# Key-value products ahead of the gate passes in the middle periods of an attention and gated-recurrence kernel

## The chip, the cores and the metric

The kernel runs on one core of a Trainium2 chip. The metric is device time in microseconds of one execution; lower is better. A core has five engines that run side by side, each through its own list of instructions in the order written, and that wait for one another by semaphores: TensorE (PE, matrix products, results in the PSUM banks), VectorE (DVE), ScalarE (ACT), GpSimd (POOL) and the DMA queues. TensorE's weight loads are shown apart from its matmuls, as PEld.

## The reference

Eight sequences of 512 rows with 128 features go through linear attention, a residual and a layer norm; then a gated recurrence runs over the eight sequences as its eight time steps, again with residual and norm.

```python
Q = elu(x @ Wq.T + bq) + 1; K = elu(x @ Wk.T + bk) + 1; V = x @ Wv.T + bv
KV = einsum('bnd,bne->bde', K, V)
Z = einsum('bnd,bd->bn', Q, K.sum(axis=1) + 1e-06)
x = layernorm(x + (einsum('bnd,bde->bne', Q, KV) / Z[..., None]) @ Wo.T + bo)
# over the first axis of x, c starts as in_c:
ft = sigmoid(xt @ wf.T + c @ uf.T + bf); it = sigmoid(xt @ wi.T + c @ ui.T + bi)
gt = tanh(xt @ wc.T + c @ uc.T + bc);    c = ft * c + it * gt
# after the last step:
h = tanh(x @ wo.T + c_final @ uo.T + bo)
out = layernorm(x + h)
```

All data are float32. The host only packs and transposes inputs.

## The kernel before

The order of every engine is written out by hand, one function per engine; no scheduler moves anything. The attention of sequence a takes, on TensorE:

- keys(a), into ps_k (line 436; for a below 4 a bias product, line 444), and queries(a), into ps_q (line 450);
- keys_x(a), line 459: the product of k_rows with the input, into small(a), a corner of the second half of ps_ctx (for a = 7 in ps_k). ScalarE copies it out (xk_copy);
- key_values(a), lines 469 and 470: two products that make the key-value matrix in small(a); VectorE adds an epsilon and writes kvo(a);
- context(a), line 479: the queries times kvo(a), into both halves of ps_ctx.

VectorE then takes the reciprocal of Z (reciprocal_z), the residual in four chunks (residual, line 1020; the upper two chunks raise y_small_ok, the lower two y_ok), the statistics, and later the normalised x1 (normalise). TensorE transposes x1(b) into ps_x1 (x1_turned, line 493); ScalarE writes its rounded part x1_hi (x1_high) and a whole copy (x1_whole), VectorE the rest x1_lo (x1_low). The gates of step t are products of a high and a low part: six matmuls on x1_hi and three on x1_lo (gates_x, lines 513 to 522), and three per gate on the state (gate_s, lines 540 to 545, which wait for s_hi from ScalarE and s_lo from GpSimd). ScalarE makes tanh of the forget gate, key_bias (the bias of the next keys), then tanh of the input and the candidate gate. VectorE makes kept_state, new_state, next_state.

The loop periods() runs six times. In one turn stand keys and queries of sequence k, the attention products of a = k - 1, the residual and norm of b = k - 2, and the gates of step t = k - 3. I call the turn in which the gates of step t stand "period t"; period 0 has an order of its own, periods 1 to 3 share one (a = 3, 4, 5), and a closing part written out by hand has the attention of 6 and 7 and the first half of the gates of step 4. From the gates of step 4 on, the 512 columns go in two halves.

TensorE's function keys_x(a) waits for x_rows_in(a), for k_ok(a + 1) and, from a = 1 to 6, for y_small_ok(a), since the corner it writes shares a bank with the context whose upper chunks the residual of a - 1 still reads. key_values(a) waits for xk_ok and k_sum_ok, context(b) for q_ok, kvo_ok and y_ok(b), x1_turned for x1_ok of each chunk, the first gate matmul for x1hi_ok.

Of the kernel before, what the change touches and what calls it, by code (L numbers as in the profile page):

```python
# [41 lines left out]
C = N // D  # L42
DZ = D + 1
H = C // 2
# [38 lines left out]
def build(nc, x, xt, w_kq, w_vo_in, w_gate, w_out, rows, att_row, out):  # L83
    with ExitStack() as ctx:
# [102 lines left out]
        ctx_mm, z_ok, y_ok = sem("ctx_mm"), sem("z_ok"), sem("y_ok")  # L187
# [230 lines left out]
        def _(pe):  # L418
# [28 lines left out]
            def queries(a):  # L447
                if a >= 1:
                    pe.wait_ge(q_relu_ok, a)
                nc.tensor.matmul(ps_q[:], wkq[:, WQ_T * D:(WQ_T + 1) * D], x_cols[:, a].rearrange("p c d -> p (c d)"),  # L450
                                 start=True, stop=True).then_inc(q_mm, 1)

            def keys_x(a):
                pe.wait_ge(x_rows_in[a], 16)
                pe.wait_ge(k_ok, a + 1)
                if 1 <= a < T - 1:
                    pe.wait_ge(y_small_ok, a)
                for c in range(C):
                    mm = nc.tensor.matmul(small(a)[:, 0:D], x_rows[:, a, c], k_rows[:, a % 2, c],  # L459
                                          start=(c == 0), stop=(c == C - 1))  # L460
                mm.then_inc(xk_mm, 1)
# [21 lines left out]
            def x1_turned(b):  # L483
                if b == 0:
                    pe.wait_ge(ident_ok, 1)
                if b >= 1:
                    pe.wait_ge(x1c_ok, b)
                for c in range(C):
                    if c in dve_chunks(b):
                        pe.wait_ge(x1_ok, x1_done(b, c))  # L490
                    else:
                        pe.wait_ge(x1_act_ok, SHARED_LN.index(b) * H + c - H + 1)
                    mm = nc.tensor.transpose(ps_x1[:, c * D:(c + 1) * D], x1[:, b, c], ident[:])  # L493
                mm.then_inc(x1t_mm, 1)
# [32 lines left out]
            def gates_x(k):  # L527
                for g in range(GATES):
                    gate_x_high(g, k)
                for g in range(GATES):  # L530
                    gate_x_low(g, k)

            def gate_s(g, k):

                ps, done = gate_bank[second_half(k)][g], gates[g][1]
                u, last, part = GATES + g, (STEPS[k][0] - 1) % 2, columns(k)
                if k == 1:
                    pe.wait_ge(split_s_lo, 1)
                pe.wait_ge(shi_ok[step_before(k)], 1)
                nc.tensor.matmul(ps[:, part], wgate_hi[:, u], s_hi[:, last, part], start=False, stop=False,  # L540
                                 skip_group_check=True)
                nc.tensor.matmul(ps[:, part], wgate_lo[:, u], s_hi[:, last, part], start=False, stop=False,
                                 skip_group_check=True)
                pe.wait_ge(slo_ok[step_before(k)], 1)
                nc.tensor.matmul(ps[:, part], wgate_hi[:, u], s_lo[:, last, part], start=False, stop=True,
                                 skip_group_check=True).then_inc(done, 1)
# [116 lines left out]
            for k, a, b, t in periods():  # L663
                if a == 0:

                    keys_x(a)
                    keys(k)
                    key_values(a)
                    queries(k)
                    context(a)  # L670
                    continue

                keys(k)
                if a == 1:
                    keys_x(a)
                if a in (2, 3):
                    x1_turned(a - 2)
                queries(k)
                if t == 0:

                    gate_x_high(0, t)
                    keys_x(a)
                    gate_x_low(0, t)
                    gate_x_high(1, t)
                    key_values(a)
                    gate_x_low(1, t)
                    gate_x_high(2, t)
                    gate_x_low(2, t)
                    context(a)
                    continue  # L690
                if t is not None:
                    gates_x(t)
                    keys_x(a)
                    gate_s(0, t)
                key_values(a)
                if a == 1:
                    setup_gates()
                if t is not None:
                    gate_s(1, t)
                    gate_s(2, t)  # L700
                context(a)
                if b >= 2:
                    x1_turned(b)

            keys(7)
            queries(7)
            gates_x(4)
            keys_x(6)
            gate_s(0, 4)
            key_values(6)  # L710
            keys_x(7)
            gate_s(1, 4)
            gate_s(2, 4)
            context(6)
            key_values(7)
            x1_turned(5)
# [40 lines left out]
        def _(act):  # L757
# [102 lines left out]
            for k, a, b, t in periods():  # L860
                if a == 0:
                    xk_copy(a)
                key_exp(k)
                if a == 1:
                    xk_copy(a)
                    act.wait_ge(halved_ok, 1)
                    nc.scalar.activation(wgate_hi[:, GATES:2 * GATES], wgate[:, GATES:2 * GATES],
                                         ACT.Copy).then_inc(split_hi, 1)
                if t is not None and t >= 1:
                    state_high(t - 1)  # L870
                if t is not None:
                    x1_whole(t)
                if a == 2:
                    xk_copy(a)
                query_exp(k)
                if b == 0:
                    first_normalise(b)
                if a == 0:

                    act.wait_ge(gate_in, 16)  # L880
                    nc.scalar.activation(wgate_hi[:, 0:GATES], wgate[:, 0:GATES], ACT.Copy).then_inc(split_hi, 1)
                if a > 2:
                    xk_copy(a)
                if t is not None:
                    forget_tanh(t)
                    key_bias(k + 1)
                    input_tanh(t)
                if b is not None:
                    x1_high(b)

            key_exp(7)
            state_high(3)
            x1_whole(4)
            query_exp(7)
            xk_copy(6)
            forget_tanh(4)
            xk_copy(7)
            input_tanh(4)
# [43 lines left out]
        def _(dve):  # L942
# [128 lines left out]
            def attention_end(b):  # L1071

                residual(b, range(H, C), y_small_ok)
                residual(b, range(H), y_ok)
                dve.wait_ge(y_ok, b + 1)
                dve.wait_ge(y_small_ok, b + 1)
                statistics(b)
                variance(b)
# [18 lines left out]
            for k, a, b, t in periods():  # L1097
                if a == 0:
                    key_values(a)
                    key_max(k)  # L1100
                    continue
                if b < 2:
                    reciprocal_z(b)
                if b == 1:
                    residual(b, range(H, C), y_small_ok)
                    x1_low(0)
                    residual(b, range(H), y_ok)
                    dve.wait_ge(y_ok, b + 1)
                    dve.wait_ge(y_small_ok, b + 1)
                    statistics(b)  # L1110
                    variance(b)
                else:
                    attention_end(b)
                if a == 1:
                    query_sum(a)
                    split_state_low()
                if a in (1, 2):
                    key_values(a)
                key_max(k)
                if a > 1:  # L1120
                    query_sum(k)
                if a > 2:
                    key_values(a)
                normalise(b)
                if a == 1:
                    split_low()
                    first_biases()
                    query_sum(k)
                if t is not None:
                    kept_state(t)  # L1130
                    new_state(t)
                    reciprocal_z(a)
                    next_state(t)
                if b >= 1:
                    x1_low(b)

            attention_end(5)
            key_max(7)
            query_sum(7)
            key_values(6)  # L1140
            normalise(5)
            kept_state(4)
            new_state(4)
            reciprocal_z(6)
            key_values(7)
            next_state(4)
            residual(6, range(H, C), y_small_ok)
            x1_low(5)
            residual(6, range(H), y_ok)
# [120 lines left out]
```

## Time and profile before

| | us |
|---|---|
| median of 3 runs | 101.58 (101.49 to 101.75) |
| the profiled execution | 101.5 |
| its span, first to last instruction | 99.4 |
| TensorE busy with matmuls | 89.9 (90%) |
| TensorE busy with weight loads | 78.3 (79%) |
| VectorE busy | 80.0 (81%) |
| ScalarE busy | 66.9 (67%) |
| GpSimd busy | 42.5 (43%) |

Times in the trace count from the span's start. Period 0 lies at 17.2 to 24.1 us, period 1 at 24.1 to 33.8, period 2 to 42.4, period 3 to 51.0, the closing part of the attention to 60.1. Matmuls are pipelined: a record ends when its results have left, while the next one has started, so starts are closer together than records are long. The chain of waits gives each piece the time by which it moved the chain on. The chain that ended last is 75% TensorE.

### The profile page before, as it was taken

The numbers are of one execution on the slowest core, as the hardware profiler recorded it, in microseconds if no ns is written. First come the engines' busy times: TensorE is split into PE (matmuls) and PEld (weight loads), VectorE is DVE, ScalarE is ACT, GpSimd is POOL, SyncE is SP. The second block draws the span as 40 slices with busy tenths as digits, with TensorE's granted clock in tenths as the row PEclk, the third lists the DMA queues.
The fourth block names the chain that finished last, engine by engine and source line by source line (L and its number), as shares of the span: only waits on it lengthen the run. The fifth ranks groups of instructions, "written<-read, shape, count | busy, mean of one in ns | idle before, by whom it ended". The sixth has DMA issues, their size and how long they took to land.

```text
span 99.4 us, 1919 instructions
## 1 busy us (share of the span) xinstructions
PE 89.9 (90%) x607; PEld 78.3 (79%) x607; DVE 80.0 (81%) x227; ACT 66.9 (67%) x139; POOL 42.5 (43%) x71
## 2 busy tenths in 40 slices
PE   5998999999999999999999999999999999979100
PEld 4868879689588968978899899999999999957000
DVE  3254499979999996899589989999767897999660
ACT  1445779479597694885869445769495787897360
POOL 3006398327258058009405802440200435788850
PEclk9999999999999999999999999999999999999995
DMA  2868999100000000000000000000000003205336
GB/s 38 306 232 300 394 399 364 48 0 3 0 0 0 0 0 0 10 0 0 0 0 0 0 0 7 3 3 0 7 0 0 0 0 106 89 24 187 129 106 211
DMA packets 5413, 7.36 MB, mean 74 GB/s; under 512 B 507, under 2 KB 3228, under 8 KB 5404
## 3 DMA queue, kind: packets, MB, share of 16 engines
q1 hardware_dynamic: 4972, 6.92, 19.8%
q10 hardware_dynamic: 432, 0.33, 1.3%
q8 instruction: 5, 0.08, 0.4%
q14 instruction: 4, 0.03, 0.1%
HBM read 5.15 MB, written 2.10 MB: 73 GB/s over the span
## 4 chain that ended last, share of the span: by engine, by line
PE 75%; POOL 9%; DVE 4%; ACT 4%; issue 4%; DVEq 0%; POOLq 0%; ACTq 0%
PE ps_k L436 7%; PE ps_ctx L459 7%; PE ps_ctx L479 6%; PE ps_q L450 6%; POOL rstd L356 6%; PE ps_x L493 4%; PE ps_f L423 4%; PE ps_f L513 2%; PE ps_ctx L469 2%; PE ps_ctx L470 2%; PE ps_f L522 2%; PE ps_c L513 1%; PE ps_c L515 1%; PE ps_f L515 1%; PE ps_i L513 1%
## 5 line engine op out<-in xcount | busy, mean ns | idle before, releaser
L375 POOL TENSOR_TENSOR s_lo<-s,s_hi 128x512 fp32r<-128x512 f32 (+1 forms) x6 | 6.7, 1110 | 24.3 <-ACT s_hi L797 24.3
L331 POOL TENSOR_TENSOR rstd<-var_eps,minus_half 128x4 f32<-128x4 f32 x8 | 8.7, 1091 | 7.8 <-DVE var_eps L996 7.8
L322 POOL TENSOR_TENSOR k_pair<-k_rows 128x256 f32<-128x256 f32 x8 | 6.3, 783 | 8.9 <-DVE k_rows L1032 8.9
L1005 DVE TENSOR_SCALAR x<-x,stats,rstd 128x128 f32<-128x128 f32 x28 | 9.8, 408 | 0.0
L846 ACT ACTIVATE x_hi<-ps_x 128x512 fp32r<-128x512 f32 x8 | 4.8, 602 | 6.4 <-PE ps_x L493 6.4
L356 POOL TENSOR_TENSOR rstd<-var_eps,minus_half 128x4 f32<-128x4 f32 (+1 forms) x9 | 8.7, 965 | 0.5
L436 PE MATMUL ps_k<-wkq,x_cols 128*128 128x128 f32 x64 | 8.7, 279 | 0.0
L767 ACT ACTIVATE k_exp<-ps_k,minus_one 128x512 f32<-128x512 f32 x8 | 5.5, 686 | 4.6 <-PE ps_k L444 3.7
L436 PEld LDWEIGHTS ps_k<-wkq,x_cols 128*128 128x128 f32 x64 | 8.2, 197 | 0.3
L450 PE MATMUL ps_q<-x_cols,wkq 128*128 128x512 f32 x16 | 8.2, 593 | 0.0
L1020 DVE SCALAR_TENSOR_TENSOR x<-ps_ctx,z_inv,x_rows 128x128 f32<-128x128 f32 x28 | 8.0, 343 | 0.1
L459 PEld LDWEIGHTS ps_ctx<-k_rows,x_rows 128*128 128x128 f32 x56 | 7.1, 191 | 1.0 <-issue 0.7
L459 PE MATMUL ps_ctx<-k_rows,x_rows 128*128 128x128 f32 x56 | 7.5, 277 | 0.4 <-DVE k_rows L1032 0.4
L479 PEld LDWEIGHTS ps_ctx<-kvo,q_cols 128*128 128x128 f32 x56 | 7.2, 191 | 0.8 <-issue 0.5
L1050 DVE SCALAR_TENSOR_TENSOR new<-th_i,th_c 128x256 f32<-128x256 f32 (+1 forms) x12 | 6.1, 510 | 2.1 <-ACT th_c L781 2.1
L479 PE MATMUL ps_ctx<-kvo,q_cols 128*128 128x129 f32 x56 | 7.5, 276 | 0.0
L1057 DVE SCALAR_TENSOR_TENSOR s<-keep,new 128x256 f32<-128x256 f32 (+1 forms) x12 | 6.2, 514 | 0.8
L990 DVE BATCH_NORM_STATS2 stats<-x 128x6 f32<-128x256 f32 x16 | 6.2, 428 | 0.2
L1032 DVE SCALAR_TENSOR_TENSOR k_rows<-k_exp,ps_k 128x512 f32<-128x512 f32 x8 | 5.5, 681 | 1.0 <-ACT k_exp L767 1.0
L772 ACT ACTIVATE q_exp<-ps_q,wkq 128x512 f32<-128x512 f32 x8 | 5.5, 687 | 0.9 <-PE ps_q L450 0.8
L823 ACT ACTIVATE x<-x,shift,rstd 128x128 f32<-128x128 f32 x13 | 5.6, 486 | 0.7 <-POOL shift L369 0.7
L797 ACT ACTIVATE s_hi<-s 128x256 fp32r<-128x256 f32 (+1 forms) x10 | 4.9, 497 | 1.7 <-DVE s L1057 1.6
(211 smaller groups left out, 284.6 us busy)
## 6 DMA issues: line engine op xcount, KB each, us to landing
x_cols<-xt SPq DMA_DIRECT2D x8, 256.0 KB, 7.3
x_rows<-x SPq DMA_DIRECT2D x8, 256.0 KB, 7.3
out<-x SPq DMA_DIRECT2D x7, 256.0 KB, 2.2
wgate<-w_gate SPq DMA_DIRECT2D x1, 384.0 KB, 6.3
out<-x SPq DMA_DIRECT2D x2, 128.0 KB, 2.0
wkq<-w_kq ACTq DMA_DIRECT2D x1, 131.0 KB, 3.4
wvo_in<-w_vo_in ACTq DMA_DIRECT2D x1, 128.0 KB, 3.3
wout<-w_out SPq DMA_DIRECT2D x1, 128.0 KB, 7.0
```

Source lines behind the costliest of these rows:

```text
L322: nc.gpsimd.tensor_tensor(k_pair[:], k_rows[:, a % 2, 0:C // 2], k_rows[:, a % 2, C // 2:C], ALU.add).then_inc(k_pair_ok, 1)
L331: nc.gpsimd.tensor_tensor(rstd[:, b], var_eps[:, b], minus_half[:], ALU.pow).then_inc(rstd_ok, 1)
L356: nc.gpsimd.tensor_tensor(part_of(rstd, u, T), part_of(var_eps, u, T), minus_half[:, 0:nt * H].rearrange("p (t c) -> p t c", c=H), ALU.pow ...
L375: nc.gpsimd.tensor_tensor(s_lo[:, t % 2, part], state(t)[:, part], s_hi[:, t % 2, part].bitcast(F32), ALU.subtract).then_inc(slo_ok[k], 1)
L436: mm = nc.tensor.matmul(ps_k[:, c * D:(c + 1) * D], x_cols[:, a, c], wkq[:, WK_T * D:(WK_T + 1) * D], start=(c == 0 and a < BIAS_BY_PE), s ...
L450: nc.tensor.matmul(ps_q[:], wkq[:, WQ_T * D:(WQ_T + 1) * D], x_cols[:, a].rearrange("p c d -> p (c d)"), start=True, stop=True).then_inc(q ...
L459: mm = nc.tensor.matmul(small(a)[:, 0:D], x_rows[:, a, c], k_rows[:, a % 2, c], start=(c == 0), stop=(c == C - 1))
L479: mm = nc.tensor.matmul(ctx_of(b, c // 2)[:, c % 2], q_cols[:, b % 2, c], kvo[:, b % 2], start=True, stop=True, skip_group_check=True)
L990: st = nc.vector.bn_stats(stats[:, b, c:c + 2].rearrange("p c m -> p (c m)"), x1[:, b, c:c + 2].rearrange("p c d -> p d c"))
L1005: nc.vector.tensor_scalar(x1[:, b, c], x1[:, b, c], mean_of(b, c), rstd[:, b, c:c + 1], ALU.subtract, ALU.mult).then_inc(x1_ok, 1)
L1020: ins = nc.vector.scalar_tensor_tensor(x1[:, b, c], ctx_of(b, c // 2)[:, c % 2, 0:D], z_inv[:, b % 2, c:c + 1], x_rows[:, b, c, 0:D], ALU. ...
L1057: nc.vector.scalar_tensor_tensor(state(t)[:, part], keep[:, part], 0.5, new[:, part], ALU.mult, ALU.add).then_inc(s_ok, 1)
```

## The change

In periods 1 to 3 and in the closing part the order within a period is written anew. On TensorE, keys_x(a) stands right behind keys(k) (in period 1 behind x1_turned(1)), key_values(a) behind queries, both ahead of all gate matmuls, which stand in one row; x1_turned(b) stands ahead of context(a). In the closing part keys_x(6) and key_values(6) are moved likewise, and keys_x(7) stands behind all gate_s of step 4.

On ScalarE, xk_copy(a) stands ahead of state_high and the query activations, x1_whole behind them. On VectorE, the residual of a is made at the end of the period itself: its upper half between reciprocal_z(a) and next_state(t), its lower half behind next_state(t), ahead of x1_low; attention_end is split, and for t of 2 and more only first_statistics is left at the next period's start. For t below 2 (and where there is no t) attention_end stays, so the residual of b = 2 stands at the start of period 1 as before. In the closing part next_state(4) stands ahead of reciprocal_z(6) and of VectorE's key_values(7).

```diff
@@ TensorE, the loop
+                if t is not None and t >= 1:
+                    keys_x(a)
                 queries(k)
...
-                if t is not None:
-                    gates_x(t)
-                    keys_x(a)
-                    gate_s(0, t)
                 key_values(a)
                 if a == 1:
                     setup_gates()
                 if t is not None:
-                    gate_s(1, t)
-                    gate_s(2, t)
-                context(a)
+                    gates_x(t)
+                    gates_s(t)
                 if b >= 2:
                     x1_turned(b)
+                context(a)
 
             keys(7)
+            keys_x(6)
             queries(7)
+            key_values(6)
             gates_x(4)
-            keys_x(6)
-            gate_s(0, 4)
-            key_values(6)
+            gates_s(4)
             keys_x(7)
-            gate_s(1, 4)
-            gate_s(2, 4)
             context(6)
@@ ScalarE, the loop
                 if t is not None and t >= 1:
+                    xk_copy(a)
                     state_high(t - 1)
-                if t is not None:
+                if t == 0:
                     x1_whole(t)
                 if a == 2:
                     xk_copy(a)
                 query_exp(k)
+                if t is not None and t >= 1:
+                    x1_whole(t)
...
-                if a > 2:
-                    xk_copy(a)
...
             key_exp(7)
+            xk_copy(6)
             state_high(3)
+            query_exp(7)
             x1_whole(4)
-            query_exp(7)
-            xk_copy(6)
@@ VectorE
                 residual(b, range(H, C), y_small_ok)
                 residual(b, range(H), y_ok)
+                first_statistics(b)
+
+            def first_statistics(b):
                 dve.wait_ge(y_ok, b + 1)
                 dve.wait_ge(y_small_ok, b + 1)
                 statistics(b)
...
+                elif t is None or t < 2:
+                    attention_end(b)
                 else:
-                    attention_end(b)
+                    first_statistics(b)
...
                     reciprocal_z(a)
+                    if t >= 1:
+                        residual(a, range(H, C), y_small_ok)
                     next_state(t)
+                    if t >= 1:
+                        residual(a, range(H), y_ok)
...
-            attention_end(5)
+            first_statistics(5)
...
+            next_state(4)
             reciprocal_z(6)
             key_values(7)
-            next_state(4)
```

TensorE in period 1, from behind keys(4), before (x1_turned(1), queries(4), the nine matmuls of gates_x(1), keys_x(3)):

```order
L493 MATMUL ps_x1<-ident,x1 128x128 x4
L450 MATMUL ps_q<-x_cols,wkq 128x512
L513 MATMUL ps_f<-x1_hi,wgate_hi 128x512
L515 MATMUL ps_f<-x1_hi,wgate_lo 128x512
L513 MATMUL ps_i<-x1_hi,wgate_hi 128x512
L515 MATMUL ps_i<-x1_hi,wgate_lo 128x512
L513 MATMUL ps_c<-x1_hi,wgate_hi 128x512
L515 MATMUL ps_c<-x1_hi,wgate_lo 128x512
L522 MATMUL ps_f<-x1_lo,wgate_hi 128x512
L522 MATMUL ps_i<-x1_lo,wgate_hi 128x512
L522 MATMUL ps_c<-x1_lo,wgate_hi 128x512
L459 MATMUL ps_ctx<-k_rows,x_rows 128x128 x4
```

and now:

```order
L493 MATMUL ps_x1<-ident,x1 128x128 x4
L459 MATMUL ps_ctx<-k_rows,x_rows 128x128 x4
L450 MATMUL ps_q<-x_cols,wkq 128x512
L469 MATMUL ps_ctx<-bias_z,k_sum 128x129
L470 MATMUL ps_ctx<-w_vo,xk 128x128
L513 MATMUL ps_f<-x1_hi,wgate_hi 128x512
```

keys_x(3) (L459) has moved over queries and nine gate matmuls, to right behind the transposition.

VectorE, now, at the end of period 0 and the start of period 1 (these rows are the same before, but for the line numbers), from new_state(0) to the statistics of b = 2:

```order
L1047 SCALAR_TENSOR_TENSOR new<-th_i,th_c 128x512
L1008 RECIPROCAL z_inv<-ps_ctx 128x4
L1054 SCALAR_TENSOR_TENSOR s<-keep,new 128x512
L1024 TENSOR_TENSOR x1_lo<-ps_x1,x1_hi 128x512
L1017 SCALAR_TENSOR_TENSOR x1<-ps_ctx,z_inv,x_rows 128x128 x4
L987 BN_STATS stats<-x1 128x6 x2
```

and now at the end of period 1, for comparison:

```order
L1047 SCALAR_TENSOR_TENSOR new<-th_i,th_c 128x512
L1008 RECIPROCAL z_inv<-ps_ctx 128x4
L1017 SCALAR_TENSOR_TENSOR x1<-ps_ctx,z_inv,x_rows 128x128 x2
L1054 SCALAR_TENSOR_TENSOR s<-keep,new 128x512
L1017 SCALAR_TENSOR_TENSOR x1<-ps_ctx,z_inv,x_rows 128x128 x2
L1024 TENSOR_TENSOR x1_lo<-ps_x1,x1_hi 128x512
L987 BN_STATS stats<-x1 128x6 x2
```

At the end of periods 1 to 3 the residual's two halves (two chunks each) have moved ahead of next_state and of x1_low; at the end of period 0 nothing has moved.

TensorE in the closing part, from the last gates_x(4) matmul on, before:

```order
L522 MATMUL ps_c<-x1_lo,wgate_hi 128x256
L459 MATMUL ps_ctx<-k_rows,x_rows 128x128 x4
L540 MATMUL ps_f<-s_hi,wgate_hi 128x256
L542 MATMUL ps_f<-s_hi,wgate_lo 128x256
L545 MATMUL ps_f<-s_lo,wgate_hi 128x256
L469 MATMUL ps_ctx<-bias_z,k_sum 128x129
L470 MATMUL ps_ctx<-w_vo,xk 128x128
L459 MATMUL ps_k<-k_rows,x_rows 128x128 x4
L540 MATMUL ps_i<-s_hi,wgate_hi 128x256
```

and now:

```order
L522 MATMUL ps_c<-x1_lo,wgate_hi 128x256
L540 MATMUL ps_f<-s_hi,wgate_hi 128x256
L542 MATMUL ps_f<-s_hi,wgate_lo 128x256
L545 MATMUL ps_f<-s_lo,wgate_hi 128x256
L540 MATMUL ps_i<-s_hi,wgate_hi 128x256
L542 MATMUL ps_i<-s_hi,wgate_lo 128x256
L545 MATMUL ps_i<-s_lo,wgate_hi 128x256
L540 MATMUL ps_c<-s_hi,wgate_hi 128x256
L542 MATMUL ps_c<-s_hi,wgate_lo 128x256
L545 MATMUL ps_c<-s_lo,wgate_hi 128x256
L459 MATMUL ps_k<-k_rows,x_rows 128x128 x4
L479 MATMUL ps_ctx<-kvo,q_cols 128x129 x4
```

keys_x(7) (into ps_k) now stands behind all nine gate_s matmuls of step 4, right ahead of context(6).

## Rows read from the trace of the kernel before

**Rows 1.** Stretches: length, busy time (count) of PE, PEld, DVE, ACT, POOL; clock, DMA.
```profile
42.37:50.98 8.61, 8.61 (x54) 7.25 (x54) 7.17 (x20) 6.25 (x11) 3.49 (x4) 1.00 0.00 0
...
60.12:77.50 17.38, 17.34 (x145) 16.82 (x144) 14.90 (x46) 11.55 (x29) 3.80 (x5) 1.00 0.01 3
92.40:97.00 4.60, 0.00 (x0) 0.00 (x0) 3.33 (x11) 2.00 (x5) 3.12 (x6) 1.00 0.34 116
97.00:99.40 2.40, 0.00 (x0) 0.00 (x0) 0.00 (x0) 0.00 (x0) 0.00 (x0) 0.52 0.65 215
```

**Rows 2.** Chain of waits, periods 1 and 3: start us, us, engine and line.
```profile
25.16 0.73 PE ps_x L493 x4
...
26.74 0.39 PE ps_f L513
...
43.26 0.86 PE ps_q L450 x2
...
45.05 0.23 PE ps_c L513
...
47.81 0.22 PE ps_ctx L469 x2
```

**Rows 3.** Instructions in order of time, TensorE, keys(7) and queries(7): start, length, line.
```profile
50.82 1.06 PE L436 MATMUL ps_k<-wkq,x_cols 128*128 128x128 f32 x8
51.71 1.02 PE L450 MATMUL ps_q<-x_cols,wkq 128*128 128x512 f32 x2
```

**Rows 4.** Instructions in order of time, VectorE, start of period 1: residual(2).
```profile
27.81 1.12 DVE L1020 SCALAR_TENSOR_TENSOR x<-ps_ctx,z_inv,x_rows 128x128 f32<-128x128 f32 x4
```

**Rows 5.** Instructions in order of time, early part: residual(0), keys_x(1), queries(2).
```profile
12.43 1.13 DVE L1020 SCALAR_TENSOR_TENSOR x<-ps_ctx,z_inv,x_rows 128x128 f32<-128x128 f32 x4
...
13.19 1.13 PE L459 MATMUL ps_ctx<-k_rows,x_rows 128*128 128x128 f32 x8
...
14.15 1.02 PE L450 MATMUL ps_q<-x_cols,wkq 128*128 128x512 f32 x2
```

**Rows 6.** Instructions in order of time, period 3: forget gate, four ScalarE instructions, VectorE.
```profile
47.42 0.39 PE L545 MATMUL ps_f<-s_lo,wgate_hi 128*128 128x512 f32 x1
...
47.85 0.69 ACT L781 ACTIVATE th_f<-ps_f,half_b 128x512 f32<-128x512 f32 x1 [0.42 <-PE ps_f L545]
48.44 0.59 ACT L837 ACTIVATE ps_k<-bk_wide 128x512 f32<-128x512 f32 x1
49.00 0.69 ACT L781 ACTIVATE th_i<-ps_i,half_b 128x512 f32<-128x512 f32 x1
49.69 0.69 ACT L781 ACTIVATE th_c<-ps_c,wkq 128x512 f32<-128x512 f32 x1
...
50.48 0.69 DVE L1050 SCALAR_TENSOR_TENSOR new<-th_i,th_c 128x512 f32<-128x512 f32 x1 [0.27 <-ACT th_c L781]
51.09 0.18 DVE L1011 RECIPROCAL z_inv<-ps_ctx 128x4 f32<-128x4 f32 x1
```

**Rows 7.** Instructions in order of time, closing part and step 5: ScalarE, VectorE, TensorE.
```profile
57.10 0.47 ACT L781 ACTIVATE th_i<-ps_i,half_b 128x256 f32<-128x256 f32 x1
57.47 0.47 ACT L781 ACTIVATE th_c<-ps_c,wkq 128x256 f32<-128x256 f32 x1
...
58.79 0.29 DVE L1091 TENSOR_TENSOR kvo<-ps_k,eps_z 128x129 f32<-128x129 f32 x1 [0.23 <-PE ps_k L470]
...
59.33 0.60 DVE L1020 SCALAR_TENSOR_TENSOR x<-ps_ctx,z_inv,x_rows 128x128 f32<-128x128 f32 x2
...
65.09 0.42 DVE L1050 SCALAR_TENSOR_TENSOR new<-th_i,th_c 128x256 f32<-128x256 f32 x1
65.61 0.43 DVE L1057 SCALAR_TENSOR_TENSOR s<-keep,new 128x256 f32<-128x256 f32 x1
...
59.23 0.68 PE L479 MATMUL ps_k<-kvo,q_cols 128*128 128x129 f32 x4
```

**Rows 8.** Instructions in order of time, TensorE, the eight matmuls of the warm-up.
```profile
1.03 3.78 PE L423 MATMUL ps_f<-ones_r 128*128 128x512 f32 x8 [1.03 <-DVE ones_r L944]
```

## The prediction

> **What bounds the kernel now.** I read first the table of stretches [rows 1]: a period of the middle is 8.61 us long and TensorE is busy for 8.61 of it, VectorE for 7.17, ScalarE for 6.25; from 60.12 to 77.50 TensorE has 17.34 of 17.38 us. Then the chain of waits [rows 2]: from 24 to 60 us it holds hardly anything but matmuls, one behind the other. So up to 77 us every microsecond in which TensorE waits is a microsecond later for all that follows, and a new order of the same matmuls can win only what it waits today: in the stretches that the change touches a few tenths (0.57 us in the closing part, 0.16 us in period 1, both below). After 77.5 us the other engines set the pace, but they start from TensorE's last gates, so a delay moves them whole. What is to be seen in the rows is therefore not who is busiest but which new wait stands in front of TensorE.
>
> **The change part by part.** No instruction is added or taken away. Four products move ahead in each period: keys_x(a), its copy, key_values(a), and on VectorE the residual. TensorE takes matmuls in the order written, so a waiting keys_x holds queries, both gate passes and the context behind it, and through them ScalarE's tanh and VectorE's state.
>
> *What keys_x waits for.* It waits on y_small_ok(a): the upper half of the previous residual, made by VectorE. Before, it stood some 3 us later, behind queries (0.86) and nine gate matmuls of 0.23 [rows 2]. The nearest row for the new place is in the early part, where keys_x stands right behind keys as it now always does [rows 5]: the residual begins at 12.43, its first two of four are done at 12.43 + 0.60 = 13.03 (0.60 for a pair in [rows 7]), and keys_x starts at 13.19. So 0.16 us from VectorE to TensorE. The same rows give the price of a restart: those eight take 1.13 us and queries starts 0.96 after their start, where a group without a wait takes 1.06 and hands over after 0.90 [rows 3]. As a running group also starts some 0.16 before the end of the one ahead, a wait costs its visible idle time and 0.24 us more.
>
> *Period 1 (a = 3).* Its residual(2) is not moved: the branch keeps attention_end for steps below 2, and the end of period 0 still has next_state and x1_low ahead of it. In the trace VectorE starts that residual at 27.81 [rows 4]; nothing it depends on is changed up to there, so the upper half is done at 27.81 + 0.60 = 28.41 and keys_x(3) starts at 28.57. TensorE is through with keys(4) and the transposition at 25.16 + 0.73 = 25.89 [rows 2]. Idle 2.68, with the restart 2.92. Given back: the first gate matmul, 0.39 instead of 0.23 today [rows 2] since it waited for x1_hi, has no wait behind such a pause, -0.16. Sum of this term: **+2.76 us**. Before, the same wait cost nothing, as keys_x(3) stood behind queries and the gates.
>
> *From one keys_x to the next, periods 1 to 3.* Here the residual's upper half is moved ahead of next_state, but it stands behind new_state, which waits for the last tanh. The loop, from the start of one keys_x: 0.96 to queries; 0.86; key_values 0.44 (two of 0.22); gates_x 9 x 0.233 = 2.10; two gate_s matmuls 0.47 [rows 2]; the third, 0.39, and 0.04 until the forget tanh starts [rows 6]: 5.26. Then tanh to key_bias 0.59, key_bias to tanh 0.56, the next tanh again 0.57 on, its own 0.69, and 0.10 to new_state: 7.77 [rows 6]. Then 0.61 to the reciprocal, its 0.18, 0.60 for two residuals, 0.16 to TensorE: **9.32 us** [rows 5 to 7]. TensorE's own work in that loop is 8.61 [rows 1]. The forget gate's matmuls end some 0.4 us later in a period than today, since gate_s(0) no longer stands ahead of key_values, and tanh, key_bias, tanh, tanh are a chain without a gap from there. Three such loops lead to keys_x(4), (5) and (6): 3 x 0.71 = **+2.14 us**. Other waits on the loop have room: the context ends about 0.4 us before the reciprocal asks for it; xk's copy is hidden by queries (0.86 against 0.28 + 0.04); VectorE has 1.4 us to spare in a period [rows 1] for statistics, keys, queries and normalising.
>
> *Closing part.* Queries(7) starts at 52.6 + 2.76 + 2.14 = 57.5 (52.6 is where it would stand with keys_x ahead and no wait). From there TensorE has 0.86 + 0.44 + 1.05 + 1.05 + 0.89 to the end of keys_x(7), its copy starts at 60.9 + 1.05 + 0.04 = 62.0. On ScalarE this copy stands between the forget and the input tanh and now has only keys_x(7) ahead of it late: input tanh 62.3, the next 0.37 on and 0.47 long, new_state at 63.2 [rows 7]. VectorE now does next_state ahead of the reciprocal and kvo(7): 0.52 for a state right behind new (65.09 to 65.61), 0.33 more, a tenth, kvo at 64.2, done 0.29 later, and 0.15 to context(7) [rows 7]: 64.6. TensorE would be there at 63.6, a new wait of 1.0 us. Today it is there at 59.23, with 0.57 us of waits on the way (queries at 51.71 [rows 3], 6.95 us of work), which go. Net **+0.4**. VectorE itself is a little less late than TensorE, as it has next_state behind it already: residual(6) 64.4 against 59.33 [rows 7], +5.1.
>
> *Behind 60 us* the order is today's. TensorE comes 5.3 us late, VectorE 5.1; one wait of TensorE for VectorE of 0.2 us closes. I take **+5.1 us** for the end: 99.4 + 5.1 = 104.5 of span, and with the 2.1 us around the span **106.6 us**. The profiled execution took 101.5 in all, the median of the runs is 101.58; what lies between is less than 0.1 us.
>
> **A rule against this reading.** TensorE's matmuls fill all 8.61 us of a period, its weight loads 7.25 [rows 1]. The Trainium skill, page "Perfetto Trace Analysis", section "Identifying the Most-Contended Engine", calls matmul busy time a poor measure of how near TensorE is to its limit and asks for the busy time of the weight loads. By that rule a period would have up to 8.61 - 7.25 = 1.36 us of room, and this is the third rival. Against it stands that the pieces of the chain, 0.23 for a gate matmul and 0.86 for queries [rows 2], add up to the whole period with nothing left over.
>
> **The rivals.** *Only the first wait is real.* If the loop's chain is shorter than its rows (the tanh overlap more, the residual is released sooner), the three loops run at TensorE's 8.61; this decides at a chain of 8.61 instead of 9.32. For it: 0.7 us is the difference of two sums of a dozen terms. Against: each term is a start-to-start time of a row. It gives 101.5 + 2.76 + 0.4 = 104.7.
>
> *The clock falls in the pause.* At the start of the trace eight gate-sized matmuls take 3.78 us, 0.47 each instead of 0.23 [rows 8]. If the pause of 2.7 us in period 1 put TensorE back to half its clock (1.2 of 2.4 GHz), about as much work would run so again: +1.9 us, 108.5. Against: at the end TensorE does nothing from 92.4 on and its granted clock is still 1.00 up to 97.0, 0.52 only after that [rows 1]. The Trainium skill, page "TensorE: Matmul & The Clock Gate", section "HAM oscillation", says that matmuls after an idle gap can start at half clock; by that rule alone this rival would be the forecast, by the trace a gap of 2.7 us is short of the 4.6 us that changed nothing.
>
> *Not slower: TensorE is not the bound.* If the dense matmuls hide room of 1.36 us a period, four periods have 5.4 us and take up the 5.1 us of waits: 101.2 to 101.8, and with the 0.57 us of the closing part perhaps 101.0. It decides at about 1.3 us a period; the idle time would then show in the records while the periods stay 8.6 us long. Against it speak the sums of the chain's pieces, above, and the copies and tanh that start 0.04 us behind the matmul they wait for [rows 6].
>
> **How the numbers follow.** Forecast 0.73, first wait alone 0.13, clock 0.06, no slower 0.05 (0.03 faster, 0.02 same), anything else slower 0.03. The forecast's own terms: first wait 2.6 to 3.0, a loop 0.5 to 0.9, closing part 0 to 1.0, so 105.7 to 107.6. With the first rival the range is 104.6 to 107.6 and leaves out under 2 in 10. About 0.3% is what a measurement of this kernel can tell from no change.
>
> **What would show it.** TensorE idle for 2.7 us ahead of keys_x(3), released by VectorE's residual, and for about 0.5 us ahead of keys_x(4), (5) and (6); periods of 9.3 us instead of 8.6; a wait of 1 us ahead of context(7) for kvo; the stretch from there to the end as long as today. I am wrong if keys_x(3) starts before 28 us, if the periods stay at 8.6 us, or if the end part shrinks by more than half a microsecond.

## The result and the profile after

The changed kernel takes 108.39 us (median of 6 runs, 108.05 to 108.91), the kernel before 101.60 us in the same comparison: ratio 1.065, interval 1.062 to 1.068. It is 6.8 us slower. The forecast was 106.6 us with a range of 104.6 to 107.6, so the sign and most of the size were right and the range was missed by 0.8 us. Three executions of the study (one of the kernel before, one in each of two experiments) ran 6 to 31 us longer at a lower clock; all medians and ratios leave them out.

TensorE's keys_x instructions in the changed kernel's trace, in order of time (start, length, engine, line, what, idle time ahead and who ended it), answer to [rows 3, 5]:

```profile
24.78 1.13 PE L436 MATMUL ps_k<-wkq,x_cols 128*128 128x128 f32 x8
25.74 0.89 PE L493 MATMUL ps_x<-ident,x 128*128 128x128 f32 x4
29.31 1.13 PE L459 MATMUL ps_ctx<-k_rows,x_rows 128*128 128x128 f32 x8 [2.67 <-DVE x L1017]
30.27 1.77 PE L450 MATMUL ps_q<-x_cols,wkq 128*128 128x512 f32 x2
...
40.27 1.13 PE L459 MATMUL ps_ctx<-k_rows,x_rows 128*128 128x128 f32 x8 [0.46 <-DVE x L1017]
...
49.59 1.13 PE L459 MATMUL ps_ctx<-k_rows,x_rows 128*128 128x128 f32 x8 [0.45 <-DVE x L1017]
...
58.90 1.13 PE L459 MATMUL ps_ctx<-k_rows,x_rows 128*128 128x128 f32 x8 [0.44 <-DVE x L1017]
...
66.87 0.68 PE L479 MATMUL ps_k<-kvo,q_cols 128*128 128x129 f32 x4 [0.74 <-DVE kvo L1091]
```

The four waits of the forecast are there, each released by VectorE's residual (line 1017), and the fifth, for kvo(7). The pause ahead of keys_x(3) is 2.67 us (forecast 2.68). From keys_x(4) to (5) and on to (6) it is 9.32 and 9.31 us (forecast 9.32). But from keys_x(3) to (4) it is 10.96, 1.64 us more than the others, and queries right behind the pause takes 1.77 instead of 1.02 us. The stretches of the trace say why (length, busy time and count of PE, PEld, DVE, ACT, POOL; granted clock; DMA), beside [rows 1]:

```profile
26.00:29.30 3.30, 0.64 (x4) 0.30 (x3) 3.29 (x9) 1.17 (x2) 0.17 (x1) 1.00 0.00 0
29.30:30.20 0.90, 0.89 (x8) 0.90 (x9) 0.87 (x4) 0.00 (x0) 0.00 (x0) 1.00 0.00 0
30.20:33.60 3.40, 3.40 (x12) 2.18 (x11) 1.18 (x4) 2.32 (x5) 2.25 (x3) 0.53 0.00 0
33.60:36.00 2.40, 2.40 (x11) 1.98 (x10) 2.27 (x6) 0.23 (x1) 1.60 (x3) 0.95 0.00 0
```

In the pause the granted clock is 1.00, and it still is while keys_x(3) runs. Then, for 3.4 us, its mean is 0.53. Shorter stretches show the fall itself:

```profile
30.30:30.60 0.30, 0.30 (x3) 0.17 (x2) 0.27 (x3) 0.12 (x1) 0.00 (x0) 0.70 0.00 0
30.60:33.50 2.90, 2.90 (x8) 1.86 (x7) 0.72 (x3) 2.09 (x5) 2.15 (x2) 0.50 0.00 0
```

A mean of 0.70 over 0.3 us puts the fall at about 30.4, some 1.1 us after work began again; from 30.6 on it is 0.50, the lower of its two levels (1.2 of 2.4 GHz). The one profile is no exception: the mean granted clock of the six runs was 0.959 to 0.974, that of the kernel before, over all its executions but the slow one, 0.973 to 0.990. Some 3.4 us at half clock in a span of 106.7 take 0.016 off the mean, about as much as these two ranges lie apart.

The profiled execution of the changed kernel has a span of 106.7 us, 7.3 more than before. Of these, 0.75 us arise ahead of everything that was changed: keys(0), at 4.61 in both traces, takes 1.91 us here and 1.22 before (shown at the end), and period 1 begins at 24.78 instead of 24.03. Without them the trace has 6.55 us, the medians 6.8. Where the medians of two kernels lie close, it helps to count from keys(4), at which period 1 begins, so that this difference drops out.

### The profile page after: what moved, and what is told of

The parts are those of the page before. It is cut to its first block, busy times and chain, and to the rows that moved or that the text cites. A ratio compares the mean times of both kernels' runs of the same rounds, so it can differ in the third digit from the quotient of the medians.

```text
span 106.7 us, 1919 instructions
## 1 busy us (share of the span) xinstructions
PE 92.6 (87%) x607; PEld 80.4 (75%) x607; DVE 83.6 (78%) x227; ACT 66.2 (62%) x139; POOL 42.8 (40%) x71
## 4 chain that ended last, share of the span: by engine, by line
PE 52%; DVE 19%; issue 9%; POOL 8%; ACT 7%; DVEq 0%; POOLq 0%; ACTq 0%
PE ps_ctx L459 6%; POOL rstd L356 6%; PE ps_q L450 6%; PE ps_k L436 4%; DVE new L1047 4%; PE ps_f L423 4%; DVE x L1002 3%; ACT th_i L777 3%; ACT th_c L777 2%; DVE x L1017 2%; DVE s L1054 2%; PE ps_ctx L479 2%; PE ps_f L513 2%; PE ps_ctx L470 1%; PE ps_ctx L469 1%
## 5 line engine op out<-in xcount | busy, mean ns | idle before, releaser
L459 PE MATMUL ps_ctx<-k_rows,x_rows 128*128 128x128 f32 x56 | 7.8, 283 | 4.4 <-DVE x L1017 4.0
L1002 DVE TENSOR_SCALAR x<-x,stats,rstd 128x128 f32<-128x128 f32 x28 | 11.0, 450 | 0.0
L459 PEld LDWEIGHTS ps_ctx<-k_rows,x_rows 128*128 128x128 f32 x56 | 6.9, 191 | 5.4 <-issue 5.3
L436 PE MATMUL ps_k<-wkq,x_cols 128*128 128x128 f32 x64 | 9.4, 294 | 0.0
L436 PEld LDWEIGHTS ps_k<-wkq,x_cols 128*128 128x128 f32 x64 | 8.8, 209 | 0.3
L450 PE MATMUL ps_q<-x_cols,wkq 128*128 128x512 f32 x16 | 8.9, 642 | 0.0
L777 ACT ACTIVATE th_f<-ps_f,half_b 128x256 f32<-128x256 f32 (+1 forms) x7 | 4.0, 569 | 7.1 <-PE ps_f L545 7.0
L1083 DVE SCALAR_TENSOR_TENSOR q_cols<-q_exp,q_relu 128x512 f32<-128x512 f32 x8 | 5.5, 684 | 2.6 <-ACT q_relu L769 2.6
L1040 DVE SCALAR_TENSOR_TENSOR keep<-th_f,s 128x256 f32<-128x256 f32 (+1 forms) x11 | 5.4, 492 | 1.8 <-ACT th_f L777 1.7
```

The costliest lines, as they stand in the source:

```text
L436: mm = nc.tensor.matmul(ps_k[:, c * D:(c + 1) * D], x_cols[:, a, c], wkq[:, WK_T * D:(WK_T + 1) * D], start=(c == 0 and a < BIAS_BY_PE), s ...
L777: nc.scalar.activation(out_tile[:, part], ps[:, part], ACT.Tanh, bias=bias, scale=scale).then_inc(ok, 1)
L1002: nc.vector.tensor_scalar(x1[:, b, c], x1[:, b, c], mean_of(b, c), rstd[:, b, c:c + 1], ALU.subtract, ALU.mult).then_inc(x1_ok, 1)
```

## Experiments

The theory after the result: **A**, the sum of the forecast holds term by term, and the missing 1.6 us are TensorE's clock, which falls because of the first pause. The rivals: the slow matmuls have another cause; the loops, not the first wait, carry the cost; VectorE's new order does it. The diffs below are excerpts. Those under "A version that beats both" are against the kernel before, the others against the changed kernel.

**Filling the first pause.** In front of keys_x(3) TensorE gets matmuls that nobody reads:

```diff
+                if t == 1:
+                    filler(11)     # 128x512 on ones_r into ps_f, after f_ok
                 if t is not None and t >= 1:
                     keys_x(a)
```

> The changed kernel with eleven extra 128x512 matmuls on constants (their result in ps_f is overwritten later) in front of keys_x(3), where TensorE stood idle for 2.67 us; at 0.233 us each they fill 2.56 us of that pause, so they cost nothing unless they end after the residual. Theory A (the pause of 2.67 us makes the granted clock fall, and the matmuls behind it lose 1.6 us): the clock stays at 1.00 from 24 to 40 us and the time falls by about 1.6 us to 106.7 us. Theory B (the slow matmuls behind the pause have another cause, such as ScalarE, VectorE and GpSimd all starting at once): the clock and the time stay where they are, 108.3 us.

Measured: 107.10 us (106.65 to 107.35), ratio to before 1.051 (1.047 to 1.055), against 1.065 without the filler. Its trace, the same stretch and the keys_x instructions:

```profile
26.00:29.00 3.00, 2.93 (x13) 2.05 (x12) 2.99 (x9) 1.18 (x2) 0.00 (x0) 1.00 0.00 0
29.00:33.60 4.60, 4.53 (x24) 3.67 (x25) 3.03 (x9) 2.55 (x5) 2.48 (x3) 1.00 0.00 0
```
```profile
26.16 2.77 PE L429 MATMUL ps_f<-ones_r 128*128 128x512 f32 x11
29.07 1.13 PE L465 MATMUL ps_ctx<-k_rows,x_rows 128*128 128x128 f32 x8
30.04 1.02 PE L456 MATMUL ps_q<-x_cols,wkq 128*128 128x512 f32 x2
...
38.39 1.13 PE L465 MATMUL ps_ctx<-k_rows,x_rows 128*128 128x128 f32 x8 [0.45 <-DVE x L1025]
```

The clock stays at 1.00 (0.983 to 0.986 as the mean of each of the four runs), queries takes 1.02 again, and the first loop is 38.39 - 29.07 = 9.32 us like the others. keys_x(3) starts no earlier, 4.52 us behind the start of keys(4) against 4.53: useless work took the place of the pause, and the kernel got 1.3 us faster by the medians (1.6 expected). Counted from keys(4) (24.55 here) to the end the trace is 80.2 us long, against 81.9 in the changed kernel, which is the 1.6 expected. That the slow matmuls come from the pause is shown, and theory B of this run falls.

**Period 1 in the old order.** TensorE and ScalarE keep the order of before in period 1 alone:

```diff
-                if t is not None and t >= 1:
+                if t is not None and t >= 2:
                     keys_x(a)
...
+                if t == 1:
+                    gates_x(t)
+                    keys_x(a)
+                    gate_s(0, t)
                 key_values(a)
```

> The changed kernel with TensorE and ScalarE in period 1 in the order of before; VectorE, periods 2 and 3 and the closing part stay changed. Theory A (the first wait costs 2.76 us and the clock 1.6 us, the loops 0.71 us each, the closing part 0.4 us): no pause ahead of keys_x(3), no fall of the clock, a short wait of 0.2 to 0.5 us ahead of keys_x(4), two loops of 9.32 us: 101.6 + 0.4 + 1.4 + 0.4 = 103.8 us. Theory B (the loops are the main cost and the fall of the clock comes by chance): over 105 us.

Measured: 104.09 us, ratio 1.021 (1.017 to 1.026), 0.3 us more than expected. Its keys_x instructions:

```profile
29.53 1.05 PE L459 MATMUL ps_ctx<-k_rows,x_rows 128*128 128x128 f32 x8
...
35.89 1.13 PE L459 MATMUL ps_ctx<-k_rows,x_rows 128*128 128x128 f32 x8
...
45.21 1.13 PE L459 MATMUL ps_ctx<-k_rows,x_rows 128*128 128x128 f32 x8 [0.45 <-DVE x L1027]
...
54.53 1.13 PE L459 MATMUL ps_ctx<-k_rows,x_rows 128*128 128x128 f32 x8 [0.45 <-DVE x L1027]
```

No pause, no fall of the clock (1.00 from 26 to 36 us), two loops of 9.32 us. The new order of this one period is worth 4.3 us of the 6.8: the first wait, 2.7, and the clock, 1.6. The loop to keys_x(4) gives nothing back. I had priced what is left of it at 0.4 us; its trace has 0.7, of which 0.4 ahead of and in the transposition, since keys(5) starts 10.00 us behind keys(4) instead of 9.57 before, and 0.3 ahead of keys_x(4), which starts 1.18 us behind keys(5) instead of the 0.89 without a wait. That is the 0.3 us by which the run came out longer.

**Residual(2) moved too.** Only VectorE: the residual of b = 2 goes to the end of period 0, as the later ones do.

```diff
-                elif t is None or t < 2:
+                elif t is None or t < 1:
                     attention_end(b)
...
-                    if t >= 1:
-                        residual(a, range(H, C), y_small_ok)
+                    residual(a, range(H, C), y_small_ok)
```

> The changed kernel with residual(2) moved as well, to the end of period 0, its upper half ahead of next_state(0). The pause ahead of keys_x(3) gets 1.2 us shorter (next_state and x1_low, 0.6 each, no longer stand ahead of it), from 2.67 to about 1.5 us. Theory A (the pause is VectorE's order, and a pause of 1.5 us leaves the clock at 1.00): 108.3 - 1.2 - 1.6 = 105.5 us. Theory B (a pause of 1.5 us is enough for the clock to fall): 107.1 us.

Measured: 105.36 us, ratio 1.034 (1.030 to 1.038). The wait and the stretch behind it:

```profile
27.23 1.13 PE L459 MATMUL ps_ctx<-k_rows,x_rows 128*128 128x128 f32 x8 [1.49 <-DVE x L1017]
28.19 1.02 PE L450 MATMUL ps_q<-x_cols,wkq 128*128 128x512 f32 x2
```
```profile
27.20:31.00 3.80, 3.77 (x21) 3.05 (x22) 3.77 (x8) 2.54 (x5) 1.63 (x2) 1.00 0.00 0
```

A pause of 1.49 us at the same place leaves the clock at 1.00. So the edit takes off 3.0 us by the medians and 2.7 by the traces, counted from keys(4): 1.2 of waiting and the clock's 1.6 with it.

**key_bias behind the tanh.** ScalarE in periods 1 to 3:

```diff
                     forget_tanh(t)
-                    key_bias(k + 1)
                     input_tanh(t)
+                    key_bias(k + 1)
```

> The changed kernel with ScalarE's key_bias behind the candidate tanh in periods 1 to 3, instead of between the forget and the input tanh. Theory A (a period is as long as the loop from keys_x over gates, tanh, new_state and the residual's upper half back to keys_x, 9.32 us): the tanh chain gets 0.5 us shorter, but the reciprocal then waits for the context, which ended 0.37 us ahead of it; so 0.33 us per loop, loops of 9.0 us, 1.0 us in all: 107.4 us. Theory B (the periods are 9.32 us long because of the restart of TensorE or another cost of the wait itself): periods stay at 9.32 us, 108.4 us.

Measured: 107.41 us, ratio 1.053 (1.048 to 1.059). Its keys_x, the clock behind the pause, and the end of the tanh chain in period 2:

```profile
28.61 1.99 PE L459 MATMUL ps_ctx<-k_rows,x_rows 128*128 128x128 f32 x8 [2.67 <-DVE x L1020]
...
39.33 1.13 PE L459 MATMUL ps_ctx<-k_rows,x_rows 128*128 128x128 f32 x8
...
48.38 1.13 PE L459 MATMUL ps_ctx<-k_rows,x_rows 128*128 128x128 f32 x8
```
```profile
28.60:29.00 0.40, 0.39 (x2) 0.40 (x3) 0.38 (x2) 0.00 (x0) 0.00 (x0) 0.59 0.00 0
29.00:32.00 3.00, 3.00 (x10) 2.06 (x10) 1.52 (x4) 0.80 (x2) 0.49 (x1) 0.50 0.00 0
```
```profile
44.60 0.69 ACT L777 ACTIVATE th_f<-ps_f,half_b 128x512 f32<-128x512 f32 x1 [1.50 <-PE ps_f L545]
...
45.58 0.39 PE L545 MATMUL ps_c<-s_lo,wgate_hi 128*128 128x512 f32 x1
...
46.01 0.69 ACT L777 ACTIVATE th_c<-ps_c,wkq 128x512 f32<-128x512 f32 x1
...
46.80 0.69 DVE L1050 SCALAR_TENSOR_TENSOR new<-th_i,th_c 128x512 f32<-128x512 f32 x1 [0.57 <-ACT th_c L777]
47.41 0.18 DVE L1011 RECIPROCAL z_inv<-ps_ctx 128x4 f32<-128x4 f32 x1
```

The loop is 9.05 us, not 9.32, though TensorE's instructions are the same: the loop goes through ScalarE and VectorE, as the forecast said. The 0.27 us are those of the tanh chain: from the forget tanh to the candidate tanh it takes 1.41 us, in the changed kernel 1.67 (45.55 to 47.22). It is not 0.5 us shorter, as I had expected, because the candidate tanh now starts 0.04 us behind the last matmul of its gate (45.58 + 0.39 = 45.97) and so waits for TensorE. The reciprocal still stands 0.61 us behind new_state, so the context did not take the place of the tanh, and that the result lies near the 9.0 foretold is luck. The pause of 2.67 us is unchanged, and so is the fall of the clock; this time it lies on keys_x(3) itself (1.99 us).

**VectorE's order alone.** TensorE and ScalarE as before, VectorE's function as changed (its diff is the one shown ahead of the prediction).

> TensorE and ScalarE as before, VectorE as in the changed kernel: the residual at the end of periods 1 to 3, and next_state(4) ahead of reciprocal_z(6) and kvo(7). Theory A (the cost comes from where TensorE asks for the residual, not from VectorE's new order): periods stay at 8.6 us, kvo(7) 0.2 us later, 101.6 to 101.9 us. Theory B (VectorE's order itself delays x1_low and the statistics so much that TensorE waits): over 102.5 us.

Measured: 102.70 us, ratio 1.007 (1.004 to 1.010), more than the 101.9 expected. The periods are 8.6 us (keys at 34.39, 42.99 and 51.60). The cost lies in the closing part: from keys(7) to context(7) it is 9.21 us (51.60 to 60.81), against 8.41 before (50.82 to 59.23). Its trace shows waits of TensorE there:

```profile
54.47 0.38 PE L522 MATMUL ps_f<-x_lo,wgate_hi 128*128 128x256 f32 x1 [0.24 <-DVE x_lo L1027]
...
56.52 0.46 PE L469 MATMUL ps_ctx<-bias_z,k_sum 128*128 128x129 f32 x2 [0.18 <-ACT xk L842]
...
60.81 0.68 PE L479 MATMUL ps_k<-kvo,q_cols 128*128 128x129 f32 x4 [0.23 <-DVE kvo L1094]
```

x1_low stands behind the whole residual now, and with the old order of TensorE the half gate pass of step 4 asks for it 0.24 us too early; I had expected the third of these waits alone. VectorE's order costs 0.7 us without TensorE's, outside the periods, so theory A holds for them and my price was too small.

**The closing part alone.** Periods as before, but for the residual of sequence 5; closing part as changed.

```diff
-                if t is not None and t >= 1:
-                    keys_x(a)
                 queries(k)
...
-                    if t >= 1:
+                    if t >= 3:
                         residual(a, range(H, C), y_small_ok)
```

> Periods 1 to 3 as before, but for the residual of sequence 5 at the end of period 3, which the closing part needs; the closing part as in the changed kernel. Theory A (closing part alone +0.4 us, and a short wait ahead of keys_x(6) of about 0.2 us idle with 0.24 us for the restart): 102.1 to 102.5 us. Theory B (the closing part costs nothing or gains, since its own waits of 0.57 us go): 101.3 to 101.7 us.

Measured: 102.18 us against 101.93 for the kernel before beside it, ratio 1.004 (1.000 to 1.009): 0.25 us by the medians, about 0.45 by the ratio, at the lower end of what theory A gives, with an interval that reaches to nothing. Its trace says more: from keys(7) to context(7) it is 9.21 us (51.09 to 60.30), 0.8 more than before, and from there to the end 0.3 less, together 0.5 us. It has the short wait ahead of keys_x(6) that was foretold:

```profile
52.33 1.13 PE L459 MATMUL ps_ctx<-k_rows,x_rows 128*128 128x128 f32 x8 [0.18 <-DVE x L1018]
```

**A version that beats both.** Three small waits of TensorE in period 1 remained in the kernel before (0.18, 0.29 and 0.16 us). VectorE stands idle in period 0 for kvo(2) while key_max(3) could run:

```diff
-                if a in (1, 2):
+                if a == 1:
                     key_values(a)
                 key_max(k)
+                if a == 2:
+                    key_values(a)
```

> The kernel before with one swap on VectorE in period 0: key_max(3) ahead of kvo(2). VectorE stands idle for 0.57 us there, waiting for TensorE's key_values(2), while key_max(3) could run since k_exp(3) was ready 1.6 us earlier. Theory A (the waits of 0.18, 0.29 and 0.16 us in period 1, ahead of keys(4), the transposition and the first gate matmul, come from this chain over key_max, key_bias, queries' sum and normalise): up to 0.6 us faster, 101.1 us. Theory B (kvo(2), 0.1 us later at most, delays context(2), or the waits have another source): no difference.

Measured: 101.38 us against 101.93, ratio 0.995 (0.992 to 0.998). Period 1 lasts from 24.11 to 33.39, 9.28 us, against 9.57 before (24.03 to 33.60):

```profile
24.11 1.06 PE L436 MATMUL ps_k<-wkq,x_cols 128*128 128x128 f32 x8
25.00 0.68 PE L493 MATMUL ps_x<-ident,x 128*128 128x128 f32 x4
25.52 1.02 PE L450 MATMUL ps_q<-x_cols,wkq 128*128 128x512 f32 x2
26.46 0.47 PE L513 MATMUL ps_f<-x_hi,wgate_hi 128*128 128x512 f32 x1
```

keys(4) no longer waits (1.06 instead of 1.13, and it starts right behind the context), the transposition waits less (0.68 instead of 0.89). The first gate matmul still waits for x1_hi. Theory A holds: 0.55 us by the medians. In the one trace 0.29 us of it are in this period and another 0.11 in period 0, where keys(4) starts 6.90 us behind keys(3) (17.21 to 24.11) instead of 7.01.

A second small move, in the closing part of the kernel before:

```diff
             gate_s(0, 4)
+            gate_s(1, 4)
             key_values(6)
             keys_x(7)
-            gate_s(1, 4)
             gate_s(2, 4)
```

> The kernel before, with one move in the closing part: the input gate's state matmuls, gate_s(1, 4), stand ahead of key_values(6), which waits there for xk's copy. Theory A (0.34 us of the 0.57 us of waits in the closing part is this wait): 0.2 to 0.4 us faster, 101.3 us. Theory B (the wait moves on to context(7), which waits for the copy and sum behind keys_x(7)): no difference.

Measured: 101.87 us against 101.72, ratio 0.999 (0.996 to 1.002): no difference to be told. In its trace the way from keys(7) to context(7) is 8.09 us (50.74 to 58.83) against 8.41 before (50.82 to 59.23), so the wait is gone. From context(7) to the end both traces have 40.2 us, so the 0.3 us reach the end there; the medians, with executions of one kernel over 1 us apart, don't show it.

> The kernel before with both small moves: key_max(3) ahead of kvo(2) on VectorE, and gate_s(1, 4) ahead of key_values(6) on TensorE. Theory A (both waits are real and add up): 0.5 us from the first, as its own run gave, and 0.3 us from the second, 101.1 us. Theory B (the second move only shifts a wait to context(7), as its own run of 0.9989 may say): as the first alone, 101.4 us.

Both moves together: 101.05 us against 101.66, ratio 0.993 (0.990 to 0.996). This is the fastest kernel of the study. By the times it stays open whether the second move gives a part of it: 0.993 and the 0.995 of the first alone lie within each other's intervals. The trace has both parts again, 9.27 us for period 1 and 8.09 from keys(7) to context(7), as each move alone.

## Why the prediction was off, point by point

| step | forecast | measured in the trace after |
|---|---|---|
| pause ahead of keys_x(3) | 2.68 | 2.67 |
| the same with the restart, up to queries(4) | 2.92 | 30.27 - 24.78 - (25.72 + 0.89 - 24.03) = 2.91 |
| keys_x(3) to (4) | 9.32 | 10.96 |
| keys_x(4) to (5), (5) to (6) | 9.32 | 9.32, 9.31 |
| keys_x(6) to context(7) | 64.6 - (57.5 - 0.96) = 8.1 | 7.97 |
| from context(7) to the end, against before | -0.2 | (106.7 - 66.87) - (99.4 - 59.23) = -0.3 |
| TensorE at half clock | 0 | +1.64 |

**Right:** what keys_x waits for, and that residual(2) had been left where it was, so that the first wait costs four times what each of the others does (2.76 against 0.71); the loop through tanh, new_state and the residual; kvo(7) in the closing part; that nearly all of it reaches the end. The runs bear each out apart: a move of residual(2) takes its part away, so does the old order in period 1, a shorter tanh chain shortens the loop, VectorE alone leaves the periods as they were. The rival that TensorE is not the bound falls: but for the 0.3 us behind context(7), no wait was absorbed.

That the loop came out to a hundredth is in part luck. Its terms are off by up to 0.04 us each way (key_bias to the input tanh 0.52 instead of 0.56, reciprocal to residual 0.21 instead of 0.18), and the 0.57 from one tanh to the next does not stand in [rows 6], which have 0.69 there, with a wait for the gate; the changed kernel's trace has the 0.57.

**Wrong:** the step that put TensorE's clock among the rivals, with a chance of 0.06, and the range that ended at 107.6, below that rival's own 108.5. Its reason was [rows 1]: TensorE idle from 92.4 to 97.0 at a granted clock of 1.00, from which I took that 4.6 us of idleness change nothing and 2.7 us less still. The changed kernel's stretches show what is wrong in that: the clock falls some time after the idleness began, here even 1.1 us after work began again, so that a row that shows 1.00 during a pause says nothing of what follows. The row of the kernel before showed just such a late fall, 0.52 from 97.0 on; I read it as a long idleness that did nothing, when there was no matmul left that it could have slowed. The price of the rival, 1.9 us from [rows 8], was near the 1.64 measured. The Trainium skill, page "TensorE: Matmul & The Clock Gate", section "HAM oscillation", says that matmuls behind an idle gap can start at half clock; the trace agrees, 0.53 for 3.4 us behind the gap, and the filled pause shows the cause. The gaps of that section's own case are longer than this one, though, so the prediction claimed too much for the page when it wrote that by its rule alone this rival would be the forecast. With the clock's part the sum is 101.6 + 5.1 + 1.6 = 108.3 against 108.39. The range was narrow by its own terms too: their bounds simply added up give 101.6 + 2.6 + 1.5 - 0.2 = 105.5 and 101.6 + 3.0 + 2.7 + 1.0 - 0.2 = 108.1, which would not have held 108.39 either.

A smaller point: the closing part was priced at +0.4 and measured by itself at 0.45 with its short wait ahead of keys_x(6) in it; VectorE's order alone was priced at about 0.2 ahead of its run and measured at 0.7.

## What to carry to other kernels

On an engine that takes its work in order and has none to spare, look up for each moved instruction when its latest input is ready by the trace, and look twice at the first and last turn of a loop, where one engine's half of a move may not have been made. Two sums of start-to-start times, one around the engine itself and one around the loop of waits, gave the new period here to a few hundredths; the longer one wins. Then ask of every long pause of TensorE whether its clock will outlive it, and count the matmuls behind the pause at half speed as a likely case, not as a remote one. Here 1.49 us did nothing and 2.67 us cost 1.6.

## What the runs showed of the hardware

A pause of 2.67 us brought TensorE's granted clock down, in two traces at different distances (1.1 us behind the pause's end in the changed kernel, right at it in the kernel with key_bias moved); pauses of 1.49 and 0.46 us at the same and the next places did not. Counted from the end of TensorE's last matmul the fall came after about 3.8 us and 2.7 us in these two, and after 4.7 us at the end of the kernel before ([rows 1], last matmul until 92.35). What a pause between 1.49 and 2.67 us does was not tried. Eleven useless matmuls in the pause made the kernel 1.3 us faster.

The first real matmuls, keys(0), take a different time from one execution to the next though nothing ahead of them differs, 1.05 to 1.91 us in the traces of this study; from those of before and of after:

```profile
4.61 1.22 PE L436 MATMUL ps_k<-wkq,x_cols 128*128 128x128 f32 x8
```
```profile
4.61 1.91 PE L436 MATMUL ps_k<-wkq,x_cols 128*128 128x128 f32 x8
```

The difference stays to the end and is some of the spread between executions of one kernel (101.4 to 102.6 us for the kernel before). The granted clock is given as 1.00 in both stretches, and also under the eight matmuls of the warm-up, which take 0.47 us each instead of 0.23 [rows 8], so at the start of a trace the lengths are the better witness.

A short VectorE instruction lasted, three times, until GpSimd's ended. In the changed kernel the variance of 128x4 stands beside s_lo and takes 1.08 us, where it took 0.17 before:

```profile
42.54 1.08 DVE L993 TENSOR_SCALAR var_eps<-stats 128x4 f32<-128x4 f32 x1
```
```profile
42.30 1.29 POOL L375 TENSOR_TENSOR s_lo<-s,s_hi 128x512 fp32r<-128x512 f32 x1 [7.02 <-ACT s_hi L793]
```

It ends at 43.62, GpSimd's at 43.59; at 51.86 and 61.19 it is the same, 0.03 us apart again. That the one holds the other up is read from these ends and was not tested. Each time new_state starts 0.10 us behind the end of the candidate tanh, so that the tanh, and not VectorE, sets its start and the long variance cost nothing here.
